# Two graph-attention layers on one core: PV in alternating column halves, x turned by VectorE, fewer instructions for K and V

## What is computed

```python
q = (x @ Wq.T).reshape(b, n, NUM_HEADS, HEAD)
k = (x @ Wk.T).reshape(b, n, NUM_HEADS, HEAD)
v = (x @ Wv.T + bv).reshape(b, n, NUM_HEADS, HEAD)
scores = jnp.einsum('bhqd,bhkd->bhqk', q, k) * scale + bias
p = jax.nn.softmax(scores, axis=-1)
out = jnp.einsum('bhqk,bhkd->bqhd', p, v).reshape(b, n, h)
x = _layernorm(x + out @ Wo.T + bo)
```

## Time and profile before

| | |
|---|---|
| runs | 2152.57 us median of 3 (2149.74 to 2153.01) |
| profiled execution, span | 2147.5 us; the page gives no separate device time of this execution |
| TensorE matmul | 2106.8 us, 98% |
| weight loads (beside matmuls) | 2008.9 us, 94% |
| VectorE | 1324.9 us, 62% |
| ScalarE | 1089.2 us, 51% |
| GpSimd | 582.5 us, 27% |
| DMA | 116.87 MB, 18.8% of 16 engines |
| mean granted clock of TensorE | 0.995 |

### The profile page before, as it was taken

How to read it: one execution, slowest core, us unless ns; L and a number is a source line. 1 busy time by engine, 2 the same in 40 slices (tenths; PEclk the granted TensorE clock), 3 DMA queues, 4 the chain that set the end, 5 groups by cost and what they waited for, 6 DMA issues and landing times.

```text
span 2147.5 us, 46614 instructions
## 1 busy us (share of the span) xinstructions
PE 2106.8 (98%) x17024; PEld 2008.9 (94%) x17024; DVE 1324.9 (62%) x2590; ACT 1089.2 (51%) x2368; POOL 582.5 (27%) x689
## 2 busy tenths in 40 slices
PE   6999999999999999999999999999999999999997
PEld 5999999999999999999999999998999999999996
DVE  6555555555554556555565555557777777777775
ACT  5555555555555555555555555554444444444443
POOL 4222222222222232222322223222232232323222
PEclk9999999999999999999999999999999999999998
DMA  7111111111111111111111111131222122222211
GB/s 201 41 51 34 49 34 38 50 34 49 34 39 49 34 49 34 45 43 34 49 35 49 39 34 49 29 76 56 74 61 81 54 81 60 75 72 63 80 54 61
DMA packets 121787, 116.87 MB, mean 54 GB/s; under 512 B 37921, under 2 KB 120609, under 8 KB 121761
## 3 DMA queue, kind: packets, MB, share of 16 engines
q1 hardware_dynamic: 121760, 116.52, 18.7%
HBM read 78.40 MB, written 25.17 MB: 48 GB/s over the span
## 4 chain that ended last, share of the span: by engine, by line
PE 95%; DVE 1%; issue 1%; ACT 1%; DMA 1%; SPq 0%; POOL 0%; POOLq 0%; DVEq 0%; ACTq 0%
PE a_bank L337 56%; PE b_bank L1094 17%; PE b_banks L1138 4%; PE b_bank L1163 4%; PE a_bank L386 3%; PE a_bank L413 2%; PE b_banks L1094 2%; PE b_banks L1149 2%; PE a_bank L399 1%; PE a_bank L423 1%; PE a_bank L440 1%; PE b_bank L1173 1%; PE b_bank L1102 1%; DMA a_bo<-in_L_gnn_bo 0%; DMA a_work<-in_L_gnn_w 0%
## 5 line engine op out<-in xcount | busy, mean ns | idle before, releaser
L738 DVE TENSOR_TENSOR a_hid_lo<-a_work,a_hid_hi 128x512 fp32r<-128x512 f32 x192 | 138.9, 724 | 409.1 <-ACT a_hid_hi L582 409.1
L337 PE MATMUL a_bank<-a_x1t_hi,a_w_hi 128*128 128x256 f32 x1152 | 328.7, 285 | 1.6 <-DVE a_x1t_lo L725 1.6
L337 PE MATMUL a_bank<-a_x1t_hi,a_w_lo 128*128 128x256 f32 x1152 | 323.9, 281 | 0.0
L337 PE MATMUL a_bank<-a_x1t_lo,a_w_hi 128*128 128x256 f32 x1152 | 323.8, 281 | 0.0
L577 ACT ACTIVATE a_work<-a_bank,a_b 128x256 f32<-128x256 f32 x384 | 161.1, 472 | 291.7 <-PE a_bank L337 290.5
L924 POOL TENSOR_TENSOR a_work<-a_work,a_gamma 128x384 f32<-128x384 f32 x128 | 151.6, 1204 | 462.7 <-DMA a_work<-in_x 438.3
L337 PE MATMUL a_bank<-a_w_hi,a_hid_hi 128*128 128x384 f32 x768 | 265.0, 345 | 1.0 <-DVE a_hid_lo L738 1.0
L337 PE MATMUL a_bank<-a_w_lo,a_hid_hi 128*128 128x384 f32 x768 | 259.0, 337 | 0.0
L337 PE MATMUL a_bank<-a_w_hi,a_hid_lo 128*128 128x384 f32 x768 | 258.8, 337 | 0.0
L337 PEld LDWEIGHTS a_bank<-a_x1t_hi,a_w_hi 128*128 128x128 f32 x1152 | 217.2, 189 | 5.6 <-DVE a_x1t_lo L725 1.8
L337 PEld LDWEIGHTS a_bank<-a_x1t_lo,a_w_hi 128*128 128x128 f32 x1152 | 217.1, 188 | 0.0
(11 more groups left out here) (168 smaller groups left out, 5928.6 us busy)
## 6 DMA issues: line engine op xcount, KB each, us to landing
a_work<-in_x SPq DMA_DIRECT2D x64, 384.0 KB, 3.4
a_work<-in_xT SPq DMA_DIRECT2D x96, 128.0 KB, 2.8
x<-a_work SPq DMA_DIRECT2D x32, 384.0 KB, 2.8
b_x<-x SPq DMA_DIRECT2D x32, 384.0 KB, 3.2
b_res<-x SPq DMA_DIRECT2D x32, 384.0 KB, 4.0
out<-b_y SPq DMA_DIRECT2D x32, 384.0 KB, 2.8
b_v_pairs<-b_v_nat SPq DMA_DIRECT2D x128, 49.5 KB, 2.7
a_work<-a_work SPq DMA_DIRECT2D x128, 49.0 KB, 1.9
```

The costliest lines, as they stand in the source:

```text
L337: r = pe.matmul(out, lhs[a], rhs[b], start=first and n == 0, stop=last and n == 2)
L738: dve.tensor_tensor(hid[1][:, p % RING, :], silu[:, p % 2, :], hid[0][:, p % RING, :].bitcast(F32), ALU.subtract).then_inc(hid_lo, 1)
```

## The change

In words, by place:
- Layer 1, TensorE's order: V of both tiles, PV of b, scores of g, transposes of ctx of b, first third of Q and K of g + 1, output projection of b, the other two thirds of Q and K of g + 1, transposes of p of g. `turn_x` is gone. PV's loops change places.
- The transposed x comes from layer 0: VectorE transposes z in blocks of 32 x 32 after `layer_norm`, SyncE stores them with eight DMAs a group (pieces of 128 bytes) in a second tensor x2T; layer 1 loads that and splits it from SBUF.
- K: two instructions of 1024 columns on VectorE.
- V and Wv have 384 columns in natural order; ones are written once into v_nat.
- The first norms of the last layer-0 group now stand before layer 1's first split on ScalarE and VectorE.
- GpSimd: `bias_res` before `root`. SyncE: swaps, load of res, load of adj, store. `norm` writes to a new tile.

```diff
     sp.wait_ge(x2_done, TILES * (g + 1))
     sp.dma_start(x2[g], z).then_inc(x2_stored, 16)
+    for t in range(TILES):
+        sp.wait_ge(turned, TILES * g + t + 1)
+        for b in range(P // 32):
+            sp.dma_start(x2T[g, t, b], z_blocks[32 * b:32 * b + 32, t, :].rearrange("p (k c) -> p k c", c=32)).then_inc(
+                x2t_stored, 16)
 
...
+    wait(dve, x2t_stored, 16 * N_TURNED * e)
+    for t in range(TILES):
+        dve.wait_ge(x2_done, TILES * e + t + 1)
+        dve.transpose(z_blocks[:, t, :], z[:, t, :]).then_inc(turned, 1)
...
+def load_xt(g):
+    wait(sp, xt_lo, g)
+    sp.dma_start(xt_raw.rearrange("p (k n) -> p k n", k=KT), x2T[g]).then_inc(xt_loaded, 16)
...
     if front and more:
-        load_x(g + 1)
+        load_xt(g + 1)
+    if front and not back:
+        sp.wait_ge(pairs_zeroed, 1)
+    if front:
+        sp.wait_ge(v_done, TILES * g + TILES)
+        wait(sp, pv_mm, TILES * (g - 1) + TILES)
+        for t in range(TILES):
+            swap_v(g, t)
     if front and not back:
         last["sync"]()
+    if back:
+        load_res(g - 1)
+    if front and more:
+        load_adj(g + 1)
     if late:
         store(g - 2)
-    if back:
-        load_res(g - 1)
-    if front:
-        for t in range(TILES):
-            swap_v(g, t)
-        if more:
-            load_adj(g + 1)
...
+def qk(g, u):
+    if u == 0:
+        pe.wait_ge(xt_lo, g + 1)
+        wait(pe, v_done, TILES * g)
+    elif u == 1:
+        wait(pe, ctx_done, TILES * (g - 1))
+    else:
+        wait(pe, y_done, TILES * (g - 1))
...
-
-        pe.wait_ge(*((q_done, 2 * (g + 2)) if t == 0 else (k_done, g + 2)))
-    for s in range(2):
-        for h in range(H1 // 2):
+        pe.wait_ge(*((k_done, g + 2) if t == 0 else (q_done, 2 * (g + 2))))
+    elif t == 0:
+        pe.wait_ge(y_done, TILES * g)
+    for h in range(H1 // 2):
+        for s in range(2):
             n = TILES * t + s
...
+    if front and t == 0:
+        pe.wait_ge(v_done, TILES * (g + 1) + 1)
...
+QK_BANK = (1, 0, 2)
+V_BANK, PV_BANK, TURN_BANK, OUT_BANK = (3, 1), (2, 0), (3, 2), (3, 2)
...
 def step(g, front=True, back=True, more=True):
     b = g - 1
     if front:
-        qk(g)
-    if back:
-        for t in range(TILES):
-            turn_p(b, t)
-    if front:
-        values(g, 0)
+        for t in range(TILES):
+            values(g, t)
     if back:
         for t in range(TILES):
             pv(b, t, front)
     if front:
-        values(g, 1)
-    if back:
-        turn_ctx(b, 0, front)
-    if front and more:
-        for t in range(TILES):
-            if back:
-                pe.wait_ge(ctx_done, TILES * b + t + 1)
-            turn_x(g + 1, t)
-    if back:
-        turn_ctx(b, 1, front)
-    if front:
         for t in range(TILES):
             scores(g, t, back)
     if back:
         for t in range(TILES):
-            attn_out(b, t, front)
+            turn_ctx(b, t, front)
+    if front and more:
+        qk(g + 1, 0)
+    if back:
+        for t in range(TILES):
+            attn_out(b, t)
+    if front and more:
+        qk(g + 1, 1)
+        qk(g + 1, 2)
+    if front:
+        for t in range(TILES):
+            turn_p(g, t)
...
+def xt_low(g):
+    dve.wait_ge(xt_hi, g + 1)
+    dve.tensor_tensor(xt[1][:].rearrange("p k n -> p (k n)"), xt_raw,
+                      xt[0][:].bitcast(F32).rearrange("p k n -> p (k n)"), ALU.subtract).then_inc(xt_lo, 1)
...
     for k in (1, 2):
-        for b in range(*SPAN1[k][:2]):
-            r = dve.tensor_scalar(k_blocks[:, :, b, :],
-                                  one[2][:, (k - 1) * GROUP:k * GROUP].rearrange("p (g n) -> p g n", g=GB),
-                                  mask[:, b:b + 1], None, ALU.mult)
+        b0, b1_, _h = SPAN1[k]
+        wide_k = [P, GB, b1_ - b0, NODES]
+        r = dve.tensor_tensor(
+            k_blocks[:, :, b0:b1_, :],
+            one[QK_BANK[2]][:, (k - 1) * GROUP:k * GROUP].rearrange("p (g n) -> p g n", g=GB).unsqueeze(2).broadcast_to(wide_k),
+            mask[:, b0:b1_].unsqueeze(1).unsqueeze(3).broadcast_to(wide_k), ALU.mult)
     r.then_inc(k_done, 1)
...
-    wait(dve, pv_mm, TILES * (g - 1) + t + 1)
-    dve.tensor_tensor(v_nat[:, t, :], one[3 if t == 0 else 0][:, 0:2 * VE],
-                      bv[:].rearrange("p r h c -> p (r h c)"), ALU.add).then_inc(v_done, 1)
+    dve.tensor_tensor(v_by_head[:, t, :, :, 0:DH1],
+                      one[V_BANK[t]][:, 0:D].rearrange("p (h r d) -> p h r d", r=2, d=DH1),
+                      bv[:].rearrange("p (h r d) -> p h r d", r=2, d=DH1), ALU.add).then_inc(v_done, 1)
...
+last["vector"][0]()
+xt_low(0)
+dve.memset(v_pairs[:], 0.0).then_inc(pairs_zeroed, 1)
 for t in range(TILES):
-    xt_low(0, t)
-last["vector"][0]()
-dve.memset(v_pairs[:], 0.0).then_inc(pairs_zeroed, 1)
+    r = dve.memset(v_by_head[:, t, :, :, DH1:VW], 1.0)
+r.then_inc(ones_set, 1)
+take_k(0)
+last["vector"][1]()
...
 def step(g, front=True, back=True, late=True, more=True):
     b = g - 1
     if front:
-        take_k(g)
-    if front and not back:
-        last["vector"][1]()
+        for t in range(TILES):
+            take_v(g, t)
+    if back:
+        for t in range(TILES):
+            take_ctx(b, t)
+    if front and more:
+        xt_low(g + 1)
     if front:
-        take_v(g, 0)
+        soften(g, 0)
     if back:
         for t in range(TILES):
-            take_ctx(b, t)
+            ctxt_low(b, t)
     if front:
-        take_v(g, 1)
+        soften(g, 1)
+        for t in range(TILES):
+            find_magnitude(g, t)
     if late:
         norm(g - 2)
     if back:
-        ctxt_low(b, 0)
+        finish(b)
     if front and more:
-        for t in range(TILES):
-            xt_low(g + 1, t)
-    if back:
-        ctxt_low(b, 1)
-    if front:
-        for t in range(TILES):
-            soften(g, t)
-        for t in range(TILES):
-            find_magnitude(g, t)
-    if back:
-        finish(b)
+        take_k(g + 1)
...
     if front:
         double_adj(g)
+    if back:
+        bias_res(g - 1)
     if late:
         root(g - 2)
-    if back:
-        bias_res(g - 1)
     if front:
         for t in range(TILES):
             shift(g, t)
```

More of the change, by code:

```diff
@@ L47 @@
 SCALE0, SCALE1 = float(DH0) ** -0.5, float(D) ** -0.5
+N_TURNED = TILES * P // 32
 def head_blocks(heads):
@@ L187, in stage, with load_piece @@
             return work[:, at:at + k * cols].rearrange("p (k c) -> p k c", k=k)
[L189 to L203, removed]
+        def load_piece(sp, piece, loaded):
+            _, dram, _, t, k, _, _ = piece
+            sp.dma_start(stage(piece), dram.rearrange("(t p) c -> p t c", p=P)[:, t:t + k]).then_inc(loaded, 16)
         def halves(piece, s):
@@ L368, in values @@
                 for k in range(KT):
-                    r = mm3(out[:, 0:2 * VE], [xt[j][:, k, t * P:(t + 1) * P] for j in range(2)],
+                    r = mm3(out[:, 0:D], [xt[j][:, k, t * P:(t + 1) * P] for j in range(2)],
                             [W["wv"][j][:, k, :] for j in range(2)], k == 0, k == KT - 1)
@@ L1122, in values @@
                     pe.wait_ge(q_done, 2 * g + 1)
-                out = one[3 if t == 0 else 0]
                 for k in range(KT):
-                    r = mm3(out[:, 0:2 * VE], [xt[j][:, k, t * P:(t + 1) * P] for j in range(2)],
+                    r = mm3(one[V_BANK[t]][:, 0:D], [xt[j][:, k, t * P:(t + 1) * P] for j in range(2)],
                             [W["Wv"][j][:, k, :] for j in range(2)], k == 0, k == KT - 1)
@@ L1304, in step @@
                         exp(g, t)
+                if front and more:
+                    take_q(g + 1, 1)
+                if front:
+                    for t in range(TILES):
+                        take_pt(g, t)
             step(0, back=False, late=False)
@@ L1380, in finish @@
                 dve.wait_ge(res_done, g + 1)
-                wait(dve, out_stored, 16 * g)
+                wait(dve, out_done, TILES * g)
                 for t in range(TILES):
                     dve.wait_ge(o_mm, TILES * g + t + 1)
-                    o = one[3] if t == 0 else two[0]
-                    dve.scalar_tensor_tensor(out=y[:, t, :], in0=o[:, 0:D], scalar=1.0, in1=res[:, t, :], op0=ALU.mult,
-                                             op1=ALU.add, accum_out=ysum[:, t:t + 1]).then_inc(y_done, 1)
+                    dve.scalar_tensor_tensor(out=y[:, t, :], in0=one[OUT_BANK[t]][:, 0:D], scalar=1.0, in1=res[:, t, :],
+                                             op0=ALU.mult, op1=ALU.add, accum_out=ysum[:, t:t + 1]).then_inc(y_done, 1)
                 dve.wait_ge(y_done, TILES * (g + 1))
```

213 lines of the change are left out of this document (95 added, 118 removed).

## The result

The changed kernel takes 2185.95 us (median of 4 runs, 2184.75 to 2186.81), the kernel before 2151.9: ratio 1.0162, interval 1.0147 to 1.0176. It is **34 us slower**, where 44 us less were forecast. Its profiled execution spans 2184.5 us.

| stretch | before | after | difference | forecast |
|---|---|---|---|---|
| layer 0, to the end of its last feed-forward matmul | 1456.3 | 1443.9 | -12.4 | -4.6 |
| from there to V of group 1 in layer 1 | 24.3 | 27.7 | +3.4 | +4.8 |
| 30 steps, V of group 1 to V of group 31 | 628.4 | 678.6 | +50.2 | -38 |
| from there to the end | 38.5 | 34.3 | -4.2 | -6 |

A forecast was written before the change was run, and what follows sets the result against it. TensorE was taken to bound the kernel (95% of the wait chain). Thirty layer-1 steps gaining 1.27 us make 38, start, layer 0, end and junction 6: 2147.5 - 44 = 2103.5, plus 5.1 gives 2108 us; range 2088 to 2138.

The forecast's parts named there:

- PV: Layer 1's PV with alternating halves: 1.52 us for 48 instructions instead of 2.41, gain 0.89 a step.
- Rival (c): Layer 1's PV gains nothing, as both halves cannot be fed at once: 2135 us, chance 0.07.
- TensorE's own sum: Layer 1's step without waits: 20.95 less PV 0.89, x transposes 0.65 and V 0.23, giving 19.18 us.
- The place of the new wait and its chain: TensorE waits for y before Q and K's third part, behind res, bias, root and norm: 0.5 us a step.
- 0.86 for the norm: Link in layer 1's chain to y: VectorE's norm after the root takes 0.86 us of 11.5.
- the clock: Lower TensorE clock after idle time, charged 2 us at the junction of the layers.
- (a): In layer 1 the load lands soon enough and y is in time: 19.18 a step, 2093 us, chance 0.22.
- (b): Layer 1's return is longer, by a later load or p's turning: 20.7 a step, 2138 us, chance 0.13.
- (d): Layer 0's writes in 128-byte pieces are dear and delay x_res: slower, 2254 us at 110 ns a packet, chance 0.05.
- Junction and end: Between layers, 4.8 us lost as norm precedes the split; at the end, 6 us gained by loading res earlier.
- Layer 0: Narrower V gains 0.08 us a step, 2.6 in 32; the turned copy of x was priced at 0.

The follow-up runs named there:

- e4: Kernel before with only layer 1's PV loops changed, to alternate between the column halves: 2123.39 us, ratio 0.9873.
- e8: Changed kernel with layer 1's V weights and the V biases padded back to their old widths by unused columns: 2199.5 us, a single run.
- e12: e7 with magnitudes found after y, plus an unused 32-byte tensor between layer 0's feed-forward weights and its activations: 2075.5 us.
- e2: Changed kernel with GpSimd taking the root before it adds the bias to res, the old order: 2128.33 us, ratio 0.9897.
- e1: Changed kernel with SyncE issuing the load of res before the wait for PV and the four swaps: 2079.53 us, ratio 0.9671.
- e6: Changed kernel with norm done by ScalarE instead of VectorE, GpSimd making one extra small product: 2114.84 us, ratio 0.9836.
- e5: Changed kernel with both the load of res before the swaps and the root before the bias: 2078.94 us, ratio 0.9666.
- e3: Changed kernel with one wait more: GpSimd's first shift waits until norm has written both tiles: 2097.17 us, ratio 0.9752.
- e7: e5 with both engines splitting xT of group 0 ahead of the last layer-0 group's norms: 2074.76 us, ratio 0.9653.
- e11: e7 with magnitudes found after y, plus an unused 32-byte tensor moving layer 0's feed-forward weights and activations together: 2066.38 us.

## Why the prediction was wrong, and where it was right

- **PV: right.** Forecast 1.52, measured 1.46, or 61 ns for each of 24 pairs; alone it is worth 27.3 us (e4). Rival (c) is out.
- **TensorE's own sum: right within 0.3.** 18.88 for 19.18. Q and K 6.44 (6.39), V 3.30 (3.31), scores 2.69 (2.75), transposes of ctx 0.63 (0.75), projection 3.13 (3.23).
- **The place of the new wait and its chain: right.** It stands before the third part of Q and K, released by y, behind res, bias and root.
- **The step that failed: "0.86 for the norm".** I took norm's time from a place where GpSimd did nothing beside it, and moved it to where it starts together with the shifts. It measured 3.07, 2.2 us more on a chain that in my own sum was already 0.5 late, so that all of it was bound to reach TensorE; only the load, 0.7 shorter than forecast, took some back. GpSimd's order was in front of me: I wrote "Shift follows the root on GpSimd" and "VectorE waits for the root (norm)" and did not put the two side by side. The kernel before even shows the effect, in a group that I had not read. Layer 1's nmean, which follows y and often meets a shift, takes 750 ns on average, layer 0's, of the same shape, 169 (VectorE's groups):

```profile
L1388 DVE TENSOR_SCALAR b_nmean<-b_ysum 128x2 f32<-128x2 f32 x32 | 24.0, 750 | 1.1
...
L806 DVE TENSOR_SCALAR a_nmean<-a_zsum 128x2 f32<-128x2 f32 x32 | 5.4, 169 | 1.1
```

- **The second step that failed: the clock.** I charged the lower clock at the junction and not in the steps, since 0.5 us of idle time did not ask for it. At 2.54 us it comes in 20 of the 29 steps and costs 1.6 us in each: 32 us of the 112 by which the 30 steps exceed TensorE's own sum.
- **Rivals.** (a) had its condition, a load that lands in 3.3 us, and y was late all the same. (b), a longer return, was the right kind and far too small (20.7 a step against 22.75); I let its price come only from the load and from turning p. The rival that I had for "slower", (d), is out: 0.52 us an issue, 1.7 us to landing, no new wait. No rival had the slower side at the place where my own chain had no room.
- **Junction and end: right in sign.** +3.4 for +4.8 and -4.2 for -6.
- **Layer 0: right in sign, wrong in size.** -12.4 for -4.6; 0.28 x 31 = 9 us of the gain come from the placement of the tensors (e8, e12), which no term of mine had.

Put together with measured terms: 30 x (18.88 - 20.95) = -62, + 73.8 idle, + 32 clock, + 6 unexplained = +50; -12.4 + 3.4 - 4.2: 37 us, the difference of the two spans (2184.5 - 2147.5).

## What to carry to other kernels

When an instruction is moved, its time in the profile is worth only what ran beside it there: look up what the engine that shares something with it does at the new place, above all where one event releases both. A wait of TensorE that comes back in every step can cost twice, for itself and for the clock behind it; here 1.35 to 1.8 us of idle time lowered the clock in 2 of 29 steps (e2), 2.3 to 2.7 in 20 of 29. And a change of several parts is worth splitting: here 27 us of gain in one loop (e4) and 106 us (e1) in the place of one load in SyncE's order lay under a result of 34 us more.

## What the hardware showed beyond what I expected

- VectorE's tensor_scalar from SBUF to SBUF is held up while GpSimd runs a tensor_tensor on SBUF: norm's two instructions take 1522 and 1623 ns beside shifts of 1472 and 1587, each ending 0.2 us behind its shift, against 474 on average in the kernel before. ScalarE's activation on the same data (e6), VectorE's reductions (e5) and its y with one input from PSUM (e3) run on.
- The granted clock fell behind idle times of 6.22 us (0.62 over the next 4.8 us) and 2.07 us (e7, 0.64) at the junction. In the steps, idle time alone does not tell: 2.65 us lowered it in one step (0.58) and not in another (1.00). It never fell behind the 0.84 to 1.22 us of e6's steps.
- How long TensorE takes depends on where the tensors lie. Moving layer 0's activations by 32 bytes against the feed-forward weights costs 0.28 us a step of 44.25 (e12), moving both together costs nothing (e11), and no wait shows in either. The 18 feed-forward matmuls behind the transposes of ctx take 2.20 us against 2.14, the other stretches change by up to 0.07 in both directions. Which distance is the best was not tried, and what lies behind it stays open.
